# Attention over 400 keys: exponentials and low halves of 1,024 columns over two score banks, with the rows' statistics, four row maxima and one wait of the keys moved

## The reference, cut to what matters

```
q  = layernorm(latents) @ Wq                   # 16 heads of 64
kv = concat(layernorm(ctx), layernorm(latents)) @ Wkv
sim  = where(mask, q @ k.T, -max)              # 32 batches x 16 heads x 64 queries x (1601 + 64) keys
attn = softmax(sim)
out  = layernorm((attn @ v) @ Wout)
```

## Time and profile before

| | |
|---|---|
| median of 3 runs | 810.05 us (809.28 to 811.12) |
| the profiled execution, its own time | 812.56 us |
| its span, first to last instruction | 810.8 us |
| mean granted TensorE clock | 0.978 |
| busy share of the span | PE 93%, ACT 75%, DVE 69%, POOL 67% |
| instructions | 22,755 |
| a pair in the loop | 44.3 us |

### The profile page before, as it was taken

How to read it: one execution, slowest core, us unless ns; L and a number is a source line. 1 busy time by engine, 2 the same in 40 slices (tenths; PEclk the granted TensorE clock), 3 DMA queues, 4 the chain that set the end, 5 groups by cost and what they waited for, 6 DMA issues and landing times.

```text
span 810.8 us, 22755 instructions
## 1 busy us (share of the span) xinstructions
PE 751.5 (93%) x7122; PEld 418.6 (52%) x7122; DVE 559.9 (69%) x1399; ACT 609.7 (75%) x1086; POOL 545.3 (67%) x745
## 2 busy tenths in 40 slices
PE   5598999999999999999999999999999999899766
PEld 3344544556464555545554655555555546455423
DVE  5776776666666767666666667676766666586677
ACT  5479788887868687888878696868788887865262
POOL 4366676686867768686868677686868686766122
PEclk9799999999999999999999999999999999999797
DMA  5303322121222202121212212121212121110001
GB/s 178 79 6 93 78 75 73 43 61 56 57 60 56 58 17 63 45 71 42 63 52 58 58 55 62 32 58 32 71 45 72 40 60 56 47 43 19 4 1 53
DMA packets 95820, 44.42 MB, mean 55 GB/s; under 512 B 66500, under 2 KB 87848, under 8 KB 95656
## 3 DMA queue, kind: packets, MB, share of 16 engines
q1 hardware_dynamic: 95728, 43.93, 19.5%
q10 hardware_dynamic: 56, 0.05, 0.0%
HBM read 24.20 MB, written 3.34 MB: 34 GB/s over the span
## 4 chain that ended last, share of the span: by engine, by line
PE 65%; DVE 14%; issue 10%; ACT 5%; POOL 3%; DMA 1%; DVEq 1%; ACTq 0%; SPq 0%; POOLq 0%
PE bank L1496 14%; PE bank L1576 7%; PE bank L1459 6%; PE bank L1463 5%; PE bank L1461 5%; PE bank L1414 4%; PE bank L1593 3%; DVE mx L1940 3%; PE bank L1431 3%; PE bank L1611 2%; PE bank L1390 2%; DVE qkl_l L1936 2%; PE bank L1430 2%; PE bank L1648 1%; ACT qkl_h L1118 1%
## 5 line engine op out<-in xcount | busy, mean ns | idle before, releaser
L867 POOL TENSOR_TENSOR p<-arena,p 128x512 f16<-128x512 f32 x256 | 297.9, 1169 | 133.0 <-ACT arena L1137 131.9
L1146 ACT ACTIVATE p<-bank,maskbias 128x512 f16<-128x512 f32 x224 | 155.2, 693 | 103.5 <-PE bank L1463 101.5
L1496 PE MATMUL bank<-p,xv 128*128 128x512 f16 (+1 forms) x768 | 182.3, 380 | 5.3 <-POOL arena L915 3.7
L1940 DVE TENSOR_REDUCE mx<-bank 128x1 f32<-128x464 f32 x256 | 154.0, 632 | 17.8 <-PE bank L1431 16.1
L1137 ACT ACTIVATE arena<-bank,maskbias 128x512 f32<-128x512 f32 x224 | 155.0, 692 | 0.0
L1496 PEld LDWEIGHTS bank<-p,xv 128*128 128x128 f16 (+1 forms) x768 | 58.2, 97 | 74.5 <-issue 25.6
L1936 DVE TENSOR_TENSOR qkl_l<-bank,qkl_h 128x512 f16<-128x512 f32 x64 | 41.1, 686 | 68.9 <-ACT qkl_h L1118 68.8
L1459 PE MATMUL bank<-qkc_h,xtT_h 128*128 128x512 f16 (+1 forms) x256 | 86.5, 389 | 0.0
L1463 PE MATMUL bank<-qkc_h,xtT_l 128*128 128x512 f16 (+1 forms) x256 | 85.0, 379 | 0.0
L1461 PE MATMUL bank<-qkc_l,xtT_h 128*128 128x512 f16 (+1 forms) x256 | 85.0, 379 | 0.0
L1431 PE MATMUL bank<-xtT_h,qkc_h 128*128 128x400 f16 x256 | 83.4, 338 | 0.0
(11 more groups left out here) (283 smaller groups left out, 1576.0 us busy)
## 6 DMA issues: line engine op xcount, KB each, us to landing
arena<-den_dram SPq DMA_DIRECT2D x62, 128.0 KB, 3.2
qkc_h<-arena SPq DMA_DIRECT2D x30, 256.0 KB, 2.4
qkc_l<-arena SPq DMA_DIRECT2D x30, 256.0 KB, 2.5
raw<-in_ctx SPq DMA_DIRECT2D x32, 192.0 KB, 2.4
lt<-lt_dram SPq DMA_DIRECT2D x60, 32.0 KB, 2.1
arena<-in_L_xattn_Wkv SPq DMA_DIRECT2D x1, 1024.0 KB, 7.8
raw<-in_ctx SPq DMA_DIRECT2D x64, 8.0 KB, 2.0
ltT_dram<-x_all SPq DMA_DIRECT2D x4, 256.0 KB, 2.8
```

The lines of the kernel that those rows point to most:

```text
L867: g.tensor_tensor(p_halves[0:r, slot, 1, :], p_all[0:r, (plan.halves_made(0, k, t) - 1) % 2, :], p_halves[0:r, slot, 0, :], ALU.subtract). ...
L1146: a.activation(p_halves[0:r, slot, 0, :], sbank[t % SRING][0:r, :], ACT.Exp, bias=bias)
L1496: op = mm(bk[:, :], halves_of[at, row, :], p_halves[at, slot, prob, :], start=tile < 2 and n == 0, stop=last and n == 2)
L1940: v.tensor_reduce(mx[:, hq_tile, part:part + 1], bk[:, 0:width], AX.X, ALU.max).then_inc(s_jobs_taken, 1)
```

## The change

A tile's two steps 2 and 3, 4 and 5, 6 and 7 of a batch become one wide unit (`wide(t)`). PE writes the scores of both steps, one behind the other, at the even step, into two banks that are now one PSUM tensor. ACT makes one high exponential of 1,024 columns and one float32 exponential of 1,024 columns, which fills both float32 buffers and counts for both steps; it waits for all low halves before it. POOL makes one subtraction of 1,024 columns. The values stay in their own steps. Steps 0 and 1 of a batch stay as they were.

Beside it, in `WINDOW` alone: the statistics move from step 4 of a batch to step 1 (k = 0) and step 0 (k = 1), that is s = 1 and 8; four of the row maxima of k = 1 move by half a step or a step; PE's wait for `kexp` moves from before the values of the step to after them. The other plan, `WHOLE`, computes what it did.

```
+    def wide(self, t):
+        return self.PAIRED and self.steps[t][1] is not None
...
-    STATS={4: (0, 4)}, AGGR=4, RSTD=5, XHAT=6, MASK=5,
+    STATS=[{1: (0, 4)}, {0: (0, 4)}, {4: (0, 4)}], AGGR=[1, 0, 4], RSTD=5, XHAT=6, MASK=5,
...
-    EVEN=dict(T=[7.5], MAX=[10.5, 11, 11, 11.5, 12, 12, 12.5, 13], MT=14.25), XV={2: (0, 4)},
+    EVEN=dict(T=[7.5], MAX=[10.5, 11, 11.5, 12, 12, 12.5, 12.5, 13], MT=14.25), XV={2: (0, 4)},
...
-        bank = [es.enter_context(nc.psum_tensor(f"bank{k}", [P, 512], F32)) for k in range(8)]
+        bank_pairs = [es.enter_context(nc.psum_tensor(f"banks{k}", [P, 1024], F32)) for k in range(4)]
+        bank = [bank_pairs[k // 2][:, 512 * (k % 2):512 * (k % 2) + 512] for k in range(8)]
+        score_pair = bank_pairs[1]
...
             def low_probs(plan, i, k, t):
-                if (k, t) in plan.SPLIT:
+                if plan.wide(t):
+                    if plan.steps[t][1] == 0:
+                        slot = slot_of(plan, k, t)
+                        pool.wait_ge(s_probs_ready, (i * 2 + k) * plan.STEPS + t + 2)
+                        g.tensor_tensor(p_halves[:, slot:slot + 2, 1, :], p_all[:, :, :], p_halves[:, slot:slot + 2, 0, :], ALU.subtract).then_inc(s_p_lo, 2)
+                elif (k, t) in plan.SPLIT:
...
+            def wide_probs(plan, i, k, t, part):
+                gg, slot, chunk = (i * 2 + k) * plan.STEPS + t, slot_of(plan, k, t), plan.chunk(plan.steps[t][0])
+                bias = maskbias[:, k, chunk:chunk + 1]
+                if part == 0:
+                    act.wait_ge(s_scores_ready, gg + 2)
+                    if happened(gg - RING + 2):
+                        act.wait_ge(s_values_done, gg - RING + 2)
+                    a.activation(p_halves[:, slot:slot + 2, 0, :], score_pair[:, :].rearrange("p (a b) -> p a b", a=2), ACT.Exp, bias=bias)
+                else:
+                    made = plan.halves_made(i, k, t)
+                    if happened(made - 1):
+                        act.wait_ge(s_p_lo, made - 1)
+                    a.activation(p_all[:, :, :], score_pair[:, :].rearrange("p (a b) -> p a b", a=2), ACT.Exp, bias=bias).then_inc(s_probs_ready, 2)
...
-                        scores(plan, i, k, t)
+                        for u in (t, t + 1) if plan.wide(t) else (t,):
+                            if not plan.wide(t) or plan.steps[t][1] == 0:
+                                scores(plan, i, k, u)
                         prep(plan, i, last, s)
-                        background(plan, i, since, s, before_self_scores)
+                        if plan is WHOLE:
+                            background(plan, i, since, s, before_self_scores)
                         if t >= LAG:
                             values(plan, i, k, t - LAG)
...
                         prep(plan, i, last, s + 0.25)
+                        if plan is WINDOW:
+                            background(plan, i, since, s, before_self_scores)
```

More of the change, by code:

```diff
@@ L171 @@
 WHOLE = Plan(0, ({0}, {0}), dict(
-    STATS={14: (0, 5), 15: (5, 9), 16: (9, 13)}, AGGR=17, RSTD=18, XHAT=20, MASK=21,
+    STATS=[{14: (0, 5), 15: (5, 9), 16: (9, 13)}] * 3, AGGR=[17] * 3, RSTD=18, XHAT=20, MASK=21,
     START=dict(QP=[-3, -3], QC=[-2, -2], QL=[-1, -1], T=[0.5, 1.5, 2.5, 3.5], MAX=[11 + m // 3 + 0.5 * (m % 3 > 0) for m in range(32)], MT=23),
@@ L1126, in rows_normalised @@
                     op.then_inc(s_xhat_ready, 1)
+            def wide_probs(plan, i, k, t, part):
[11 more added lines that the diff above has]
+                    a.activation(p_all[:, :, :], score_pair[:, :].rearrange("p (a b) -> p a b", a=2), ACT.Exp, bias=bias).then_inc(s_probs_ready, 2)
             def probs(plan, i, k, t, part):
+                if plan.wide(t):
+                    if plan.steps[t][1] == 0:
+                        wide_probs(plan, i, k, t, part)
+                    return
                 b = i * 2 + k
@@ L1885, in ahead @@
                 at, CH = plan.at, plan.CH
-                if t in at["STATS"]:
-                    if t == min(at["STATS"]):
+                which = 2 if isinstance(n, int) and n < 2 else par
+                if t in at["STATS"][which]:
+                    if t == min(at["STATS"][which]):
                         dve.wait_ge(s_ctx_loaded[par], ctx_count(plan, n, par))
@@ L1890, in ahead @@
                             dve.wait_ge(s_ctx_rstd, n)
-                    for c in range(*at["STATS"][t]):
+                    for c in range(*at["STATS"][which][t]):
                         v.bn_stats(st[:, c, :], raw[:, par, c, :])
-                if t == at["AGGR"]:
+                if t == at["AGGR"][which]:
                     dve.drain()
```

## The result

| | before | after |
|---|---|---|
| median of 4 runs each | 810.38 us (809.28 to 811.12) | 884.72 us (883.65 to 888.84) |
| ratio after to before | | 1.093 (95%: 1.089 to 1.097) |
| the profiled execution, its own time | 812.56 us | 885.14 us |
| its span | 810.8 us | 883.4 us |

The change makes the kernel 9.3% slower. The forecast was slower too, but at 867 us, and the measured time lies just above its range of 836 to 884 us.

A forecast was written before the change was run, and what follows sets the result against it. PE was taken as the bound, other engines having one step of slack. Pairs 1 to 14 add 54.0 us, pair 0 1.6, the last about 1: 56.6 on 812.56 gives 869.2, less 2.5 for the median: 867 us, range 836 to 884.

The forecast's parts named there:

- The walk through the loop pair: Loop pair, stretch by stretch between even steps: +3.86 us a pair, giving 48.15 us; chance 0.70.
- 2-3: Steps 2 and 3: next scores wait for the wide float32 exponential on ACT; 3.88 us becomes 4.71, +0.83.
- 4-5: Steps 4 and 5: values of step 2 wait 0.45 us for the wide low half; +0.42 us.
- 12-13: Steps 12 and 13: P1 behind the wide low half on POOL delays XH and the row maxima; +2.23 us.
- 14-15: Steps 14 and 15: T waits for ACT's normalising, now behind both wide exponentials; +1.56 us.
- PE's idle time before scores, put down to the float32 exponential: Sign to look for in the trace: some 0.5 us a pair in place of nothing.
- 3 us a pair at most: PE's waits before the change: for DVE's row maxima, the maxima's copy and the spread keys, over ten pairs.
- Pair 0 has no P1 behind it: 1.6. The last has no row maxima, T or normalising in its second half: about 1.: First and last pairs: added cost 1.6 us and about 1 us; pairs 1 to 14 carry 54.0 us.
- The statistics lie in DVE's idle time. 0.: Steps 8-9: nothing wide, the low half before is in time, the moved statistics cost nothing; 0 us.
- the waits chain further, or the clock falls: Rival: late maxima delay further jobs, or PE gets half its clock; 885 us and more; chance 0.10.
- one of the two large waits is not there: Rival: P1's wait at steps 12-13 is hidden, 836 us, or T's at 14-15 is covered, 844; chance 0.13.
- PE stays the bound, and the change pays: Rival: waits at steps 2, 4, 12 and 14 are covered, three gains remain, 18 us; 792 us; chance 0.06.

The follow-up runs named there:

- g1_stats_alone: Kernel before the change with only the statistics moved to steps 1 and 8: 827.3 us, ratio 1.021.
- j2_wide_in_loop: Changed kernel with wide units only in pairs 2 to 14, narrow steps in pairs 0, 1 and 15: 869.0 us, ratio 1.072.
- e4_no_wide: Changed kernel with nothing wide; statistics, row maxima and wait for the spread keys as in the change: 834.6 us, ratio 1.028.
- g2_maxima_alone: Kernel before the change with only the row maxima of k = 1 moved: 830.3 us, ratio 1.025.
- h2_old_maxima: Changed kernel with the row maxima of k = 1 back at their old steps: 878.8 us, ratio 1.084.
- e6_paired_scores: Changed kernel with both steps' scores one behind the other on PE, but narrow exponentials and narrow low halves: 858.8 us, ratio 1.060.
- j1_batch3_late: Changed kernel with the statistics of batch 3 alone back at step 4: 881.5 us, ratio 1.087.
- e1: Changed kernel with the statistics in pairs 0 and 1 kept at step 4 of a batch, as before: 881.6 us, ratio 1.086.
- e2: Changed kernel with P1 moved from step 11 to step 10, ahead of the wide low half: 876.4 us, ratio 1.082.
- e5: Changed kernel with wide exponentials but each low half subtracted by itself, 512 columns at a time: 879.5 us, ratio 1.086.
- g4: Changed kernel with the statistics back at step 4 of each batch: 907.3 us, ratio 1.120.
- e3: Changed kernel with the reciprocal deviations and the normalising one step earlier: 873.3 us, ratio 1.078.
- h1: Changed kernel with P1 at step 10, odd batches' RSTD and normalising one step earlier, statistics of batches 2 and 3 at step 4: 850.0 us, ratio 1.048.

## Why the forecast was right in direction and short in size

**The walk through the loop pair held in its sum.** For pair 7, measured and forecast by stretch: steps 0-1 6.67 and 6.55; 2-3 4.69 and 4.71; 4-5 5.94 and 5.96; 6-7 6.01 and 5.94; 8-9 7.99 and 7.84; 10-11 4.76 and 4.71; 12-13 6.15 and 6.50; 14-15 5.89 and 5.94. The sum is 48.09 against 48.15 us. The largest error is step 12, where the last maxima came 0.3 us sooner. Against the loop's mean of 44.49 us before (its first pairs are longer than pair 7) the increase is 3.60 us a pair and not 3.86: 46.8 us in place of 50.2, a term 3.4 us too large. Three of its readings were less right than the sum. The sign "PE's idle time before scores, put down to the float32 exponential" did not show: no score matmul waited, and PE's longest waits of steps 2 and 3 are for DVE's maxima, a line that the forecast's list of waits did not have there. Steps 2 to 3 would have grown by the statistics alone (4.75 us in g1_stats_alone), so their hit is partly luck. And the waits of the earlier trace rows make 3.4 us a pair, where the forecast says "3 us a pair at most".

**The step that failed is the last one of the walk**: "Pair 0 has no P1 behind it: 1.6. The last has no row maxima, T or normalising in its second half: about 1." With pair 1 at 3.9 these ends were to cost 6.5 us; they cost 25.8, 19.3 more; with the 3.4 too many in the loop the profiled execution is 15.9 us above its forecast of 869.2. (The forecast then took off 2.5 us for the median, and the change's profiled execution lay only 0.4 above its own: the rest of the 17.7 us.) It failed in two ways.
- "The statistics lie in DVE's idle time. 0." In the loop of the wide kernel they cost next to nothing (0.15 us in steps 8 to 9, and steps 2 to 3 are as long without them). It is wrong for pair 0, where the load has only just been issued. I had counted DVE's time, not when its input lands, nor what stands behind it in DVE's queue. Early statistics cost some 8 us up to pair 2 (8.2 in g1_stats_alone, 8.1 in j2_wide_in_loop).
- The wide units cost more in the ends (against j2_wide_in_loop 4.8 us in pair 0, 5.9 in pair 1, 9.7 from pair 15 on; against e4_no_wide 4.3, 5.5 and 7.6) than in a loop pair (2.6, after against e4_no_wide). The same kind of wait is there, and a stretch of half clock behind one: steps 12 to 13 of the last pair took 7.19 us, with PE waiting 1.21 us for XH and then three score matmuls in 1.3 us in place of 0.65. Its very last low half held the values 2.29 us with nothing else to do. Which share each wait has was not measured place by place, so why the ends pay more than the loop for the same unit stays open in part.

**The rival that came nearest** was "the waits chain further, or the clock falls", given 0.10: not through 15 pairs as I had priced it, but in three of them. The rival "one of the two large waits is not there" is refuted by the chain above. "PE stays the bound, and the change pays" does not hold even with both large waits mended (850.0 us).

**Costs seen apart.** The moved maxima were costed at nothing, as part of stretches 10 to 13; alone they cost 19 us (g2_maxima_alone), in the wide kernel 6 (after against h2_old_maxima). My sum was right there only because the walk let PE meet them in place. P1 was given the whole of step 12's 2.2 us and had 1.05 with the moved maxima beside it, and at most 0.4 without them (steps 12 to 13 of h2_old_maxima). In the whole pair the moved maxima have 0.4 (after against h2_old_maxima).

**The two rules.** The Trainium skill ("PSUM — Partial Sum Buffer", summary rules) asks for another bank for the matmul than the one being read. No run here shows what it costs when there is none: neither in the changed kernel nor with paired scores (e6_paired_scores) did the scores' matmuls wait for an exponential.
A wide exponential took 1.11 us, and the next instruction started 1.01 us after it (391.20 to 392.21 in pair 7), 0.13 us less than two narrow spacings of 0.57. An estimate by the Trainium skill ("ScalarE: Activation LUTs", rules for kernel authors) is 1.15 us for one and a saving of 0.3 for the pair. The first agrees. The second is more than twice what is measured: narrow exponentials of 0.69 us start 0.57 us apart, so they overlap, and the estimate counts each in full. ACT's measured busy time fell by 32 us, without use.

## What to carry to other kernels

Joining two double-buffered steps into one wide instruction saves little on its engine and delays what stands behind it in that engine's queue: here PE, the bound, lost time where values waited for a wide low half, where P1 stood behind one, and where the normalising stood behind the wide exponentials. Two causes in one stretch can each be enough (steps 2 to 3) or need each other (P1 and the maxima), so the difference of two runs is a price only beside everything that both have. Cost a moved step by walking every queue it enters, and do it again for the first and last iterations written out beside the loop: here an input had only just been requested there, and half the clock followed the hole. Take such a change apart before judging it; of the three small parts here one was a small gain, and two that cost 16 and 19 us alone cost less, or paid, beside the others.

## What was not expected of the hardware

PE can be granted half its clock in the midst of full work. In j1_batch3_late, at the start of pair 14 (columns as above):

```profile
713.60:715.20 1.60, 1.60 (x12) 0.67 (x12) 1.11 (x5) 0.87 (x3) 1.60 (x2) 1.00 0.42 155
715.30:718.70 3.40, 3.40 (x25) 2.56 (x26) 0.89 (x2) 2.39 (x4) 3.15 (x7) 0.51 0.75 209
718.80:720.00 1.20, 1.20 (x12) 0.46 (x10) 0.31 (x1) 0.61 (x2) 0.17 (x1) 1.00 0.01 2
```

PE was busy before it and through it; the last hole was its wait of some 1.5 us for T, which ended about 2 us earlier (T began at 713.51). The step from 0 to 1 took 4.84 us there and 3.19 in the other pairs. The profiled executions of e1, e2, e5, g4, h2, j1 and j2 have one to four such pairs in the loop, at step 0, on another pair each time (g4 has three, and seven more stretches at its other wait, at step 13). All of them have T's wait. The narrow kernels, and e3, e6 and h1, where T waits 0.7 us (e6) or not at all, have none; nor has the changed kernel's own execution, which does have the wait. So in these runs the hole seems to be needed, and not to be enough. What decides between one pair and the next stays open. The one shown is worth 1.65 us (4.84 less 3.19), a noise that a kernel without the hole did not show.
